# A graph and expert kernel: the second pass's plan work, its end and its first turned rows put in another order

## The reference

```
x = x + gcn2(layernorm(x))           # two graph convolutions, weights W1, W2, biases b1, b2
x = x + moe0(layernorm(x)[None])     # routing on the MEAN row: two of 8 experts for all rows
x = x + gat(layernorm(x))            # graph attention, 4 heads
x = x + moe1(layernorm(x)[None])     # two of 8 experts per row
```

```
logits = jnp.mean(x, axis=1) @ Wr + br
```

## Time and profile before

| | us |
|---|---|
| median of 3 timed runs | 1689.72 |
| lowest and highest of them | 1688.8, 1691.82 |
| the profiled execution, its own time | 1685.19 |
| its span, first to last instruction | 1683.5 |
| mean granted TensorE clock in it | 0.863 |

### The profile page before, as it was taken

The page is one execution under the profiler, slowest core; times in us unless marked ns, Lnnn a source line. Parts: engine busy times, 40 slices in busy tenths (PEclk is TensorE's granted clock), DMA queues, the critical chain, the costliest instruction groups (busy, mean ns, idle before and its releaser), DMA issues.

```text
span 1683.5 us, 24383 instructions
## 1 busy us (share of the span) xinstructions
PE 1294.3 (77%) x7016; PEld 910.2 (54%) x7017; DVE 923.2 (55%) x1923; ACT 574.6 (34%) x1254; POOL 713.6 (42%) x777
## 2 busy tenths in 40 slices
PE   2566778998998899998166676777667766599997
PEld 1544545665655566666133444444444456589896
DVE  6988885675245752344355555555555496523332
ACT  1778885000000323233033333333333424123222
POOL 5400000222233000012777777777775660356763
PEclk9867567999999999999588888888888976699999
DMA  4110000000200200001444443443443015478885
GB/s 133 41 30 0 0 0 0 1 1 7 77 10 1 74 1 13 13 19 38 123 110 109 109 110 108 109 109 108 110 109 86 26 59 173 146 189 212 205 209 125
DMA packets 80560, 130.58 MB, mean 78 GB/s; under 512 B 16408, under 2 KB 49845, under 8 KB 80324
## 3 DMA queue, kind: packets, MB, share of 16 engines
q0 software_dynamic: 31712, 71.66, 17.5%
q10 hardware_dynamic: 15848, 29.56, 5.8%
q1 hardware_dynamic: 32892, 28.00, 5.2%
HBM read 110.38 MB, written 18.80 MB: 77 GB/s over the span
## 4 chain that ended last, share of the span: by engine, by line
PE 49%; POOL 15%; issue 11%; DVE 10%; DMA 7%; ACT 4%; POOLq 1%; ACTq 1%; DVEq 0%; SPq 0%
POOL mem L809 12%; PE ps L1253 12%; PE ps L1209 7%; PE ps L1409 6%; PE ps L1329 5%; PE ps L1315 5%; DMA mem<-table,mem 4%; DMA out_dram<-mem 3%; PE ps L1528 3%; PE ps L1542 3%; PE ps L1376 1%; PE ps L1414 1%; ACT mem L1051 1%; POOL mem L829 1%; PE ps L1348 1%
## 5 line engine op out<-in xcount | busy, mean ns | idle before, releaser
L809 POOL DMA_INDIRECT mem<-table,mem x391 | 370.9, 949 | 119.1 <-issue 109.1
L1409 PE MATMUL ps<-mem 128*128 x832 | 290.2, 447 | 7.1 <-issue 2.1
L779 POOL TENSOR_SCALAR mem<-mem 128x128 f32<-128x128 f32 x100 | 71.8, 730 | 401.8 <-ACT mem L946 217.0
L1253 PE MATMUL ps<-mem 128*128 128x384 bf16 x1250 | 221.1, 334 | 7.3 <-DMA mem<-L_gnn_b_dram 3.6
L1051 ACT ACTIVATE mem<-ps x416 | 162.3, 390 | 182.6 <-PE ps L1409 154.3
L1209 PE MATMUL ps<-mem 128*128 128x200 bf16 x792 | 140.5, 341 | 65.8 <-issue 51.9
L1409 PEld LDWEIGHTS ps<-mem 128*128 128x128 f32 x832 | 145.9, 218 | 73.4 <-issue 48.2
L1253 PEld LDWEIGHTS ps<-mem 128*128 128x128 f16 x1250 | 125.5, 101 | 91.9 <-issue 6.0
L1209 PEld LDWEIGHTS ps<-mem 128*128 128x128 bf16 x792 | 92.1, 116 | 114.5 <-issue 98.7
L1376 PE MATMUL ps<-mem 128*16 128x128 f32 x100 | 25.1, 405 | 148.1 <-ACT mem L1063 148.1
L2012 DVE TENSOR_TENSOR mem<-mem,ps 128x1024 f32<-128x1024 f32 x98 | 113.0, 1215 | 32.5 <-ACT mem L1072 32.5
(11 more groups left out here) (463 smaller groups left out, 2098.8 us busy)
## 6 DMA issues: line engine op xcount, KB each, us to landing
mem<-L_ffn_W_dram ACTq DMA_DIRECT2D x56, 512.0 KB, 4.3
mem<-table,mem POOLq DMA_INDIRECT x395, 2.8
mem<-x_dram SPq DMA_DIRECT2D x8, 640.0 KB, 9.4
mem<-L_ffn_W_dram SPq DMA_DIRECT2D x4, 1024.0 KB, 6.9
out_dram<-mem SPq DMA_DIRECT2D x6, 512.0 KB
xn_d<-mem SPq DMA_DIRECT2D x6, 512.0 KB, 3.0
table<-mem SPq DMA_DIRECT2D x5, 528.0 KB, 3.0
mem<-L_ffn_W_dram SPq DMA_DIRECT2D x4, 512.0 KB, 6.0
```

Of the source, the lines that this page charges most:

```text
L809: pool.indirect_dma_start(ring[:, t % RING, :], None, table3[:, :], bass.IndirectOffsetOnAxis(ap=IDX[:, t:t + 1], axis=0)).then_inc(row_in ...
L1253: ins = pe.matmul(ps[:, (n * VB + v) % 2, 0:3 * HID], adj[:, v * ABLK + hi * P:v * ABLK + (hi + 1) * P], HS[n][:, hi, :, :].rearrange("p t ...
L1409: pe.matmul(flat[:, bass.ds(bank, ROW)], OH[:, q % 2, s, :], ringW[:, bass.ds(slot, ROW)], start=False, stop=False, skip_group_check=True) ...
```

## The change

Four things. The plan work is cut into parts and dealt out over blocks 15 to 21, each behind the finishes and statistics of its block instead of in front of them; the signal `plan_ready` comes at the end of block 21. The bias rows of the groups 3 and 4 are added at the end of blocks 13 and 14, those of groups 0 to 2 where they were. The square root and the reciprocal of the first 16 row blocks are taken inside the pass (ACT between its copies of row blocks 21 and 22, DVE in block 23), so that the chunks 0 and 1 can be normalised between the last finishes, and chunks 2 and 3 straight after them; the other nine blocks have a square root of their own, on ACT behind its copies of chunks 0 and 1. TensorE turns chunks 0 and 1 before it forms the plan's products, and chunks 2 to 6 after them.

```diff
+SOON = 4 * 4
@@ scalar
                 act.activation(AT[:, b * P:(b + 1) * P], ps[:, 4 + b % 4, 0:P], ACT.Copy).then_inc(z_taken, 1)
-
-            act.wait_ge(var_ready, 2)
-            act.activation(rstd[:, :], mv1[:, :, 1], ACT.Sqrt, bias=eps[:, 0:1]).then_inc(std_ready, 1)
+                if b == NB - 4:
+                    act.wait_ge(var_ready, 2)
+                    act.activation(mv1[:, 0:SOON, 1], mv1[:, 0:SOON, 1], ACT.Sqrt, bias=eps[:, 0:1]).then_inc(std_ready, 1)
+
             for c in range(len(CH)):
+                if c == 2:
+                    act.wait_ge(var_ready, 3)
+                    act.activation(rstd[:, SOON:NB], mv1[:, SOON:NB, 1], ACT.Sqrt, bias=eps[:, 0:1]).then_inc(std_ready, 1)
                 for k in range(2):
@@ tensor
+            def turn_rows(c):
+                pe.wait_ge(ln_ready, len(CH) + c + 1)
+                for k in range(2):
+                    if c:
+                        pe.wait_ge(xt_ready, 2 * len(CH) + 2 * (c - 1) + k + 1)
+                    for b in range(CH[c]):
+                        ins = pe.transpose(ps[:, k, b * P:(b + 1) * P], XN[:, C0[c] + b, k * P:(k + 1) * P], ident[:, :])
+                    ins.then_inc(tr_ready, 1)
+
+            turn_rows(0)
+            turn_rows(1)
             pe.wait_ge(o_taken, NB)
             pe.wait_ge(plan_ready, 1)
...
             ins.then_inc(plan_ps, 1)
-            for c in range(len(CH)):
...
+            for c in range(2, len(CH)):
+                turn_rows(c)
@@ vector
+            def add_bias(g):
+                dve.wait_ge(x_in[g], 64 if g == NG - 1 else 32)
+                xg = X[:, g * GB:(g + 1) * GB, :]
+                ch.link(dve.tensor_tensor(xg, xg, b2bc[:, :].unsqueeze(1).broadcast_to([P, GB, D]), ALU.add))
+
             def finish2(b):
-                if b % GB == 0:
...
+                if b % GB == 0 and b // GB < 3:
+                    add_bias(b // GB)
@@
+            def plan_compare(marks, at, op):
+                for i in range(CMPW):
+                    ch.mark(dve.tensor_scalar(marks[:, i * STEPS:(i + 1) * STEPS], iotaK[:, :], at[:, i:i + 1], None, op))
+
+            def normalise(c):
+                for b in range(C0[c], C0[c] + CH[c]):
+                    factor = mv1[:, b, 1:2] if b < SOON else rstd[:, b:b + 1]
+                    ins = dve.tensor_scalar(XN[:, b, :], X[:, b, :], mv1[:, b, 0:1], factor, ALU.subtract, ALU.mult)
...
             for v in range(VB):
                 gather_parts(1, v)
-                if v == 15:
-                    plan_steps()
-                if v == 18:
-                    plan_flags()
-                if v == 20:
-                    plan_rows()
...
+                if v in (13, 14):
+                    add_bias(v - 10)
+                elif v == 15:
+                    plan_bounds()
+                elif v == 16:
+                    plan_from()
+                elif v == 17:
+                    plan_upto()
+                elif v == 18:
+                    plan_flags()
+                elif v == 19:
+                    plan_rows()
+                    plan_compare(CGE, PVI, ALU.is_ge)
+                elif v == 20:
+                    plan_compare(CEQ, PVI, ALU.is_equal)
+                elif v == 21:
+                    plan_compare(CEN, PVN, ALU.is_equal)
+                    dve.wait_ge(dve_op, ch.value())
+                    dve.nop().then_inc(plan_ready, 1)
+                    dve.nop().then_inc(var_ready, 1)
+                elif v == 23:
+                    dve.wait_ge(std_ready, 2)
+                    ch.link(dve.reciprocal(mv1[:, 0:SOON, 1], mv1[:, 0:SOON, 1]))
             rest = SECOND[VB - 1] + list(LEFT)
-            for b in rest:
-                finish2(b)
-                if b > rest[0]:
-                    stats_of(b - 1)
+            finish2(NB - 4)
+            normalise(0)
+            stats_of(NB - 4)
+            finish2(NB - 3)
+            finish2(NB - 2)
+            normalise(1)
+            stats_of(NB - 3)
+            stats_of(NB - 2)
+            finish2(NB - 1)
             stats_of(NB - 1)
             dve.wait_ge(dve_op, ch.value())
             spread_of(SECOND[VB - 2] + rest)
             dve.wait_ge(dve_op, ch.value())
             dve.nop().then_inc(var_ready, 1)
             dve.nop().then_inc(x_ready, NG)
-            dve.wait_ge(std_ready, 2)
-            ch.link(dve.reciprocal(rstd[:, :], rstd[:, :]))
+            normalise(2)
+            normalise(3)
+            dve.wait_ge(std_ready, 3)
+            ch.link(dve.reciprocal(rstd[:, SOON:NB], rstd[:, SOON:NB]))
             ch.link(dve.tensor_tensor(rstd[:, NB - 1:NB], rstd[:, NB - 1:NB], endc[:, 3:4], ALU.mult))
...
+            for c in range(SOON // 4, len(CH)):
+                normalise(c)
```

More of the change, by code:

```diff
@@ L1765, in spread_of, with plan_bounds @@
                     ch.mark(dve.bn_aggr(mv1[:, b, :], stats1[:, b, :]))
-            def plan_steps():
+            def plan_bounds():
                 dve.wait_ge(plan_pads, 6)
@@ L1778, in plan_steps, with plan_from, plan_upto @@
                 ch.link(dve.tensor_tensor(tlo[:, :], EPV[:, :], tcol[:, :], ALU.add))
+            def plan_from():
                 for c in range(EC):
                     ch.mark(dve.tensor_scalar(S[:, c, :], iotaK[:, :], tlo[:, c:c + 1], None, ALU.is_ge))
+            def plan_upto():
                 dve.wait_ge(dve_op, ch.value())
@@ L1797, in plan_rows @@
                 ch.link(dve.tensor_scalar(PVN[:, :], PVI[:, :], -1.0, None, ALU.add))
[L1798 to L1802, removed]
+            def plan_compare(marks, at, op):
[5 more added lines that the diff above has]
+                    ins = dve.tensor_scalar(XN[:, b, :], X[:, b, :], mv1[:, b, 0:1], factor, ALU.subtract, ALU.mult)
+                    if b < C0[c] + CH[c] - 1:
+                        ch.mark(ins)
+                ins.then_inc(ln_ready, 1)
             for v in range(VB):
                 gather_parts(1, v)
-                if v == 15:
-                    plan_steps()
-                if v == 18:
-                    plan_flags()
-                if v == 20:
-                    plan_rows()
                 if v == 7:
@@ L1821, in _ @@
                         stats_of(b)
-            rest = SECOND[VB - 1] + list(LEFT)
-            for b in rest:
-                finish2(b)
-                if b > rest[0]:
-                    stats_of(b - 1)
+                if v in (13, 14):
[21 more added lines that the diff above has]
+                    ch.link(dve.reciprocal(mv1[:, 0:SOON, 1], mv1[:, 0:SOON, 1]))
+            rest = SECOND[VB - 1] + list(LEFT)
+            assert rest == [NB - 4, NB - 3, NB - 2, NB - 1]
+            finish2(NB - 4)
[7 more added lines that the diff above has]
+            finish2(NB - 1)
             stats_of(NB - 1)
```

4 lines of the change are left out of this document (removed).

## The result

| | before | after |
|---|---|---|
| median, 6 runs each | 1688.24 us | 1676.57 us |
| lowest and highest | 1685.38, 1691.82 | 1673.41, 1678.79 |
| span of the profiled execution | 1683.5 us | 1671.7 us |

The ratio is 0.993, 95% interval 0.9913 to 0.9947: faster by 11.7 us, with 9 to 15 inside the interval. Timed again on another chip it was 0.9941 (0.9927 to 0.9955, 9.9 us).

The account below looks back on a forecast made before the run. TensorE waits in the second pass for DVE's plan work, which delays row finishes. Gains of 7.6 us in the pass and 1.2 in the tail, 8.8 off the 1689.72 median, gave 1680.9 us; range 1677.5 to 1685.0.

Parts of the forecast that it names:

- The pass: Second pass, blocks 15, 20 and the one after: TensorE losses of 1.18, 4.87 and 1.53 go, together 7.6 us.
- The bound per block: DVE work per block fits TensorE's 5.23 us; the dearest, block 19, takes 4.99, with 0.24 to spare.
- full 13.9 us: Plan work on DVE that would show in full without the cover of TensorE's 5.23 us per block.
- The tail: From the pass's end to the mean: products start later, two chunks fewer remain; gain 1.2 us, bounds -0.5 to +2.7.
- I take the tail's mixture as before: TensorE clock between last projections and mean assumed unchanged, so the plan's products keep their 4.27 us.
- Rival (c): Between last projections and mean, transposes fill the sparse stretch and keep 2.4 GHz: 1.5 us more gain, 1679.4; 15%.
- What follows the mean (routing, experts) hangs on it and shifts as it stands: Everything behind the mean was forecast to move earlier unchanged, keeping its 1117 us.
- (a): Turned rows do not keep TensorE's clock up before the mean: 3.9 us off the gain, 1684.8; 8%.
- (b): Stretch before the mean gives nothing, finish 24 and products coming later by what two chunks save: 1682.1; 15%.
- (d): Plan work not all hidden in the pass: late in block 19 or DVE stopped by a wait; 1682 to 1685; 7%.
- (f): Change does not act, the waits at the projections having a cause other than plan work: 1689.7; 2%.
- (e): POOL's pick pairs slow beside DVE's comparisons in blocks 15 to 21, making the kernel slower: 1693; 3%.

Follow-up runs that it names:

- the first experiment: Kernel before with only the plan work dealt out over blocks 15 to 21 behind the finishes; ratio 0.9972 (0.9961 to 0.9984).
- the filled tail: Kernel before plus nine 384-column matmuls, results unused, in TensorE's idle time among the last projections; ratio 0.9996 (0.9985 to 1.0007).

## Why the prediction was right, and where it was wrong

**The pass: right.** 7.6 forecast, 7.61 measured, with its three parts. The bound per block held too: 4.99 us of DVE work in block 19 against 5.23, and 0.23 to spare in the row, 0.24 in the forecast. The "full 13.9 us" of plan work is a slip, since its parts as listed there make 16.7 (one of the three calls of eight comparisons is left out); nothing hangs on it. That an overrun there would be cheap, which was only argued, the first experiment shows with 6.45 us.

**The tail: the step that failed** is "I take the tail's mixture as before", that is, the 4.27 us for the products. Counted from the projection of block 24, I had projection 24 done and the turning of the first chunk begun at 4.18 (measured 4.18), the last finish ending at 6.3 (6.25), the products starting at 6.9 (6.62). But the products take 2.93 us, not 4.27, since TensorE is at 2.4 GHz. With 0.26 from the earlier start and some 0.1 behind, the gain is 2.98 and not 1.2. The earlier start is a slip in the sum: 550.8 and two chunks at 1.5, less a copy of 0.60, make 553.2 and not 553.5.

Rival (c) had the full clock, at 15%, with the reason that transposes fill the sparse stretch. The runs bear out that the turned rows are part of it. With rows turned ahead of them the products take 1.62 in all eight traces, whatever the clock did ahead of the pass. The changed kernel's second trace has the clock at half where both traces of the kernel before have it, and yet 1.62 against 2.95; and with the products first the half clock is back. But DVE's normalising makes the gaps longer there than in the kernel before, so it isn't told what the gaps do and what the turned rows do. Whether the stall of block 21 has a part too stays open: the three traces with 1.62 and no row turned ahead (the plan work alone twice, the filled tail) are also those whose clock took another course before any edit acts. What exactly the clock answers to was not settled.

**Behind the mean: also missed.** "What follows the mean (routing, experts) hangs on it and shifts as it stands" left out one microsecond. The expert products took 207.4 us in both traces of the kernel before and 206.4 in all three of the changed kernel. At their start the clock fell before and did not after (a microsecond in each kernel, before and after; columns as in the earlier trace rows):

```profile
581.00:582.00 1.00, 1.00 (x2) 0.34 (x1) 1.00 (x2) 0.46 (x1) 0.00 (x0) 0.50 0.89 274
```

```profile
569.00:570.00 1.00, 1.00 (x4) 0.29 (x2) 1.00 (x2) 1.00 (x1) 0.00 (x0) 1.00 0.97 310
```

The other traces warn against giving this microsecond to the change. The kernel with the plan parts in front of the finishes has the changed kernel's pass and tail, and its experts took 208.8; the kernel with two pairs of banks had 206.4 in one trace and 208.6 in the other. With that microsecond counted the change brings 7.6 + 3.0 + 1.0 = 11.6 us by the traces, without it 10.6; the two timings say 11.7 and 9.9. The 1.7 us ahead of the first projection and the 1.5 lost behind the experts, in code that the change doesn't touch, are left out as noise.

**The range: too narrow at its lower end.** It had the tail's upper bound (2.7), but was anchored to a median of three runs, 1689.72, which six runs put at 1688.24, and had nothing for the clock elsewhere. The 4.3 us between the forecast and the median measured are 1.5 of anchor, 1.8 of tail and 1.0 behind the mean, the last of which may be chance. The forecast's 8.8 off the better anchor would have been 1679.4.

**The rivals.** (a), turned rows that let the clock down, is wrong: in eight traces with rows turned ahead of the products those run at 2.4 GHz, and 16.82 comes four times. The Trainium skill's sentence, in "TensorE: Matmul & The Clock Gate", Part 4, that full clock doesn't engage for transposes, since they don't count as busy in the same way, would have the tail at half clock; no trace here agrees. (b), (d) and (f) did not come. (e): POOL's pairs took 1.18 to 1.36 in blocks 15 to 22. With the plan parts in front of the finishes they took 1.50 to 2.04, still far from 5.23. The Trainium skill's "GPSIMD Engine Reference", Specifications, says that GpSimd shares its SBUF interfaces with VectorE, with contention when DVE runs in a 2-port mode or with two SBUF inputs. The direction agrees: a pair is slower where DVE's plan work runs beside it, 4.82 at the worst. Which of the two conditions it was, no run here shows.

## What to carry to other kernels

Side work that an engine does in one lump stalls its partner by what goes beyond the slack per step; cut it so that each piece fits the slack, and where in the step it stands mattered nothing here (pieces of up to 3.5 us in steps of 5.23). Before adding up a tail, look at the clock of each of its pieces, and cost both levels: here that one choice was 1.3 us, more than the whole gain forecast for the tail (1.2). Before you read a change of the clock as the work of an edit, look whether the clock ran alike ahead of it: two traces of one kernel can agree and still differ from another kernel's by chance. Look also for a finish that stands behind a reduction it doesn't need: one line moved there took 5.1 us from the pass.

## What the runs showed of the hardware

Where TensorE's clock falls is repeatable only in part. The kernel before and the changed kernel have the same tail and the same time in the experts in each of their traces (207.4 and 206.4 us). The kernel with two pairs of banks has not: 206.4 and 208.6 us in the experts. Ahead of the change it varies too: from the start of the first pass to the first projection, with the same code in all kernels, the traces have 155.9 to 156.0 five times, 157.6 to 157.8 seven times, 159.2 and 159.7 once each. One place is the start of the second pass, some 27 us ahead of the first projection. The grant is 0.50 there in both traces of the kernel before and in the second of the changed kernel, and 1.00 in the other eleven. The rows are of the kernel before (first projection at 438.44), of the changed kernel's second trace (460.25) and of the first with the plan work alone (437.72), in windows of a microsecond:

```profile
411.00:412.00 1.00, 1.00 (x4) 0.45 (x3) 0.00 (x0) 0.00 (x0) 0.00 (x0) 0.50 0.00 0
```

```profile
433.00:434.00 1.00, 1.00 (x5) 0.49 (x4) 0.00 (x0) 0.00 (x0) 0.00 (x0) 0.50 0.00 0
```

```profile
410.00:411.00 1.00, 1.00 (x8) 0.60 (x7) 0.24 (x1) 0.00 (x0) 0.00 (x0) 1.00 0.00 0
```

Such steps of about 1.7 us may be a good part of the 5 to 6 us by which the six runs of one kernel differ; only the profiled run of each has a trace, so that is not shown. A trace cut into stretches tells tenths where the whole time tells three microseconds.

TensorE keeps the full clock on turned rows alone: in the kernel before, from 556.5 to 565.8, it did nothing else (eight 128x128 transposes in 1.14 us and 0.35 of waiting, in turn), at a grant of 1.00.
